# Projected query and key chunks by way of DRAM, a new layout of queries and keys, and another place for Wo in the last batch

## The chip, the cores and the metric

The kernel runs on one core of a Trainium2 chip. The metric is the device time of one execution, in microseconds (us), and the figure given is the median of the runs. A run of this kernel is timed to about 0.1%: its three runs lie between 1504.58 and 1505.42 us.

## The reference

One transformer layer, post-norm, on X of 4 batches x 1024 tokens x 512 channels, float32: causal attention with 16 query heads and 8 key/value heads of 64 (two query heads share one key/value head), rotary embedding on q and k, scores capped by a tanh, then an int8-quantised linear layer, each followed by a residual and a layer norm.

```python
q = q * cos + _rotate_half(q) * sin
k = k * cos + _rotate_half(k) * sin
att = jnp.einsum('bhqd,bhkd->bhqk', q, k) * 256.0 ** (-0.5)
att = SOFTCAP * jnp.tanh(att / SOFTCAP)
att = softmax(where(causal, att, -inf))
x = _layernorm(x + (att @ v).reshape(b, t, NH * HD) @ Wo)
q8, in_scale = per_token_quant_int8(x)
x = _layernorm(x + float16((q8 @ weight.T) * in_scale * w_scale + bias))
```

## The kernel before, in words

Precision: each large float32 operand is split in a high part, rounded to float32r, and a low part, the rest; a product is then two or three float32r matmuls.

The work goes by batch b (4) and, inside a batch, by unit u (4). A unit is two key/value heads with their four query heads; units are numbered m = 4b + u through the kernel (16). Three chunks of a unit are projected: x = 0 is k for all 1024 tokens, x = 1 and 2 are q for the first and the second 512. PE projects a chunk (`project`, L655), DVE applies the rotary embedding (`rope_read`, L1076 to L1091), ACT rounds the high part (`round_rope`, L901), DVE makes the low part (`rope_low`, L1097). The parts stand in `work_r`, two places that chunks use in turn. From there they must reach `qk` on other partitions: a score matmul contracts over 128 partitions that hold high and low parts of q below each other, against k copied twice. `put` (L400) does that with eight DMAs for one part of one chunk: L418 for k (32 partitions x 1024 elements, 128 KB each), L427 for q (32 x 512, 64 KB each). `qk` has two halves of 32 KB per partition, for even and odd units.

Attention of a unit takes 18 steps s, nine for each key/value head. At a step PE computes 2 banks of scores (`score`, L709), ACT does tanh and exp (L914, L919), POOL masks (L1317), DVE splits the probabilities (L1109, L1113), and PE weighs v with them three steps later (`weigh`, L735). Sums and outputs leave by ACT (L933), which has two buffers in turn, and by a store to `y_scratch` on SP's queue (`put_sums`, L507). The projections of the next unit lie between the steps. The orders of all engines are written out by hand; waits are on semaphores. `turns` and `chunk_at` say at which step which chunk is read, rounded and put; in the last unit of a batch they come one or two steps later.

At the end of a batch the divisors are read back (`load_div`, L456), inverted, stored (`store_inverse`, L462), read as rows (`load_rows`, L471), spread over partitions by PE (L755), and y, read back in tiles (`load_y`, L448), is scaled and multiplied with Wo (`project_out`, L777), followed by norms and the linear layer. Wo, high and low part of 2 MB each, is read from `wo_scratch`: the high part at step 11 of the last unit (L589), since it lies on the place of the first head of odd units in `qk`, the low part after the last score (L603). At the same time v of the next batch is projected (`project_v`, L677), whose weights `load_wv` (L495) brings, and x of the next batch is loaded and split in unit 2 (`load_x_turned`, L436; `split_x`, L864 and L1051).

SP issues nearly all DMAs, one after the other, and its waits stand in the same row. At the end of batches 0 to 2 ACT issues one put of eight. In the first batch `wo` is first made in `qk`'s odd half and stored (L554, L558), so puts of unit 1 wait for that (L406).

## Time and profile before

| what | value |
|---|---|
| median of 3 runs | 1504.92 us |
| the profiled execution's own time | 1501.25 us |
| its span, first to last instruction | 1499.3 us |
| PE busy (matmul) | 1322.7 us, 88% |
| DVE, ACT, POOL busy | 1096.8, 849.1, 380.8 us |
| granted TensorE clock, mean | 0.936 of full speed |
| DMA | 196.22 MB, mean 131 GB/s |
| longest DMA waits of PE | 28.4 us for qk, 31.4 us for rows |

The span is one execution, and the profiled one was shorter than the median of the runs by 3.67 us. Busy time says how much an engine did, not whether it set the time: for this the profile has the waits (who waited for whom), the timeline, and the chain of work that ended last, followed back from the last instruction. SPq and ACTq are the two queues on which DMAs are issued; an issue there occupies the queue, and the landing comes later.

### The profile page before, as it was taken

To read this page: it belongs to the slowest core of one execution; us is meant where nothing else is said; L and a number is where in the kernel's file an instruction comes from. 1 tells how busy PE (TensorE), PEld (TensorE's weight loads), DVE (VectorE), ACT (ScalarE), POOL (GpSimd) and SP (SyncE) were. 2 spreads that over 40 slices of the span, in tenths; PEclk is the share of its full clock that TensorE was granted. 3 is DMA by queue.
4 is the path that set the end of the run, shared out by engine and by line. 5 is a ranking of instruction groups with operands and counts; after the bars stand their busy time and mean duration, and the time that the engine had idled before them with its cause. 6 is when DMAs were issued, how large, how long until landed. Compare 5 with 4: busy or idle time off the path is not lost.

```text
span 1499.3 us, 17504 instructions
## 1 busy us (share of the span) xinstructions
PE 1322.7 (88%) x5824; PEld 963.7 (64%) x5840; DVE 1096.8 (73%) x1367; ACT 849.1 (57%) x952; POOL 380.8 (25%) x448
## 2 busy tenths in 40 slices
PE   6479999978988999897886999999599799999695
PEld 5357777656655777675664777767476477777463
DVE  4369888863677888885486888888258788888485
ACT  4167687752236777764223777687123577779232
POOL 2231111102552111110265112111036312111165
PEclk9789999989988999998998999999799899999896
DMA  7766445474513454547341454446642154343541
GB/s 280 261 205 160 103 129 144 113 211 123 156 50 87 115 139 109 155 96 244 95 133 47 98 137 117 103 144 186 181 123 78 56 137 103 102 110 103 149 109 42
DMA packets 120765, 196.22 MB, mean 131 GB/s; under 512 B 26466, under 2 KB 68964, under 8 KB 116836
## 3 DMA queue, kind: packets, MB, share of 16 engines
q1 hardware_dynamic: 114916, 185.14, 44.2%
q10 hardware_dynamic: 5760, 9.97, 2.0%
q8 instruction: 46, 0.75, 0.2%
q14 instruction: 43, 0.35, 0.1%
HBM read 89.39 MB, written 38.54 MB: 85 GB/s over the span
## 4 chain that ended last, share of the span: by engine, by line
PE 62%; DVE 10%; DMA 9%; SPq 7%; issue 5%; ACT 3%; POOL 3%; ACTq 1%; DVEq 0%; POOLq 0%
PE ps L735 21%; PE ps L655 15%; PE ps L709 14%; PE ps L777 6%; PE ps L677 4%; SPq L427 4%; DMA y_scratch<-sums 3%; DMA rows<-r_scratch 2%; DVE prob_hi L1109 1%; ACT probs L914 1%; DVE stats L1195 1%; DVE probs L1174 1%; DMA qk<-work_r 1%; DMA r_scratch<-inverse 1%; POOL rstd L1332 1%
## 5 line engine op out<-in xcount | busy, mean ns | idle before, releaser
L735 PE MATMUL ps<-prob_hi,v 128*65 128x512 f32 (+3 forms) x1280 | 415.1, 374 | 3.3 <-DVE prob_lo L1113 3.3
L914 ACT ACTIVATE probs<-ps 128x1024 f32<-128x1024 f32 x288 | 293.6, 1020 | 161.9 <-PE ps L709 159.2
L709 PE MATMUL ps<-qk 128*128 128x512 f32 (+1 forms) x1280 | 322.9, 379 | 54.2 <-DMA qk<-work_r 28.4
L1113 DVE TENSOR_TENSOR prob_lo<-probs,prob_hi 128x1024 fp32r<-128x1024 f32 x288 | 360.1, 1250 | 9.9
L1317 POOL TENSOR_SCALAR_AFFINE_SELECT probs<-probs 128x256 f32<-128x256 f32 (+1 forms) x192 | 145.3, 765 | 808.0 <-ACT probs L919 808.0
L919 ACT ACTIVATE probs<-probs 128x1024 f32<-128x1024 f32 x288 | 305.6, 1061 | 8.8
L709 PEld LDWEIGHTS ps<-qk 128*128 128x128 f32 x1280 | 230.1, 193 | 116.9 <-ACT probs L914 27.9
L655 PE MATMUL ps<-xT,w_ring 128*128 128x512 f32 x1152 | 293.5, 399 | 10.0 <-DVE xT L1051 8.0
L1109 DVE CAST prob_hi<-probs 128x1024 fp32r<-128x1024 f32 x288 | 206.3, 716 | 118.5 <-POOL probs L1317 69.6
L655 PEld LDWEIGHTS ps<-xT,w_ring 128*128 128x128 f32 x1152 | 219.6, 193 | 58.3 <-DVE xT L1051 9.3
L735 PE MATMUL ps<-prob_lo,v 128*65 128x512 f32 (+1 forms) x640 | 239.2, 374 | 0.0
L735 PEld LDWEIGHTS ps<-prob_hi,v 128*65 128x65 f32 (+1 forms) x1280 | 173.0, 136 | 92.5 <-DVE prob_lo L1113 5.7
L777 PE MATMUL ps<-wo,y_hi 128*128 128x512 f32 x512 | 184.9, 434 | 11.4 <-POOL y_lo L1323 11.4
L933 ACT ACTIVATE sums<-ps 65x512 f32<-65x512 f32 x128 | 74.7, 584 | 104.9 <-PE ps L735 87.7
L777 PEld LDWEIGHTS ps<-wo,y_hi 128*128 128x128 f32 x512 | 102.7, 205 | 48.0 <-POOL y_lo L1323 17.5
L677 PE MATMUL ps<-w_v,xT 128*128 128x512 f32 x384 | 97.9, 413 | 39.7 <-issue 27.9
L735 PEld LDWEIGHTS ps<-prob_lo,v 128*65 128x65 f32 x640 | 87.6, 137 | 51.6 <-issue 2.0
L1323 POOL TENSOR_TENSOR y_lo<-y_raw,y_hi 128x1024 fp32r<-128x1024 f32 x32 | 76.2, 2381 | 155.0 <-ACT y_hi L941 155.0
L677 PEld LDWEIGHTS ps<-w_v,xT 128*128 128x128 f32 x384 | 76.7, 202 | 58.7 <-issue 42.1
L777 PE MATMUL ps<-wo,y_lo 128*128 128x512 f32 x256 | 112.5, 439 | 0.0
L961 ACT ACTIVATE q16T<-ps 128x512 bf16<-128x512 bf16 x32 | 19.1, 597 | 112.2 <-PE ps L787 112.2
L941 ACT ACTIVATE y_hi<-y_raw 128x1024 fp32r<-128x1024 f32 x32 | 33.8, 1057 | 74.8 <-DVE y_raw L1137 74.8
(77 smaller groups left out, 1042.9 us busy)
## 6 DMA issues: line engine op xcount, KB each, us to landing
qk<-work_r SPq DMA_DIRECT2D x256, 128.0 KB, 2.3
qk<-work_r SPq DMA_DIRECT2D x488, 64.0 KB, 2.0
y_scratch<-sums SPq DMA_DIRECT2D x128, 130.0 KB
wo<-wo_scratch SPq DMA_DIRECT2D x8, 2048.0 KB, 7.8
y_raw<-y_scratch SPq DMA_DIRECT2D x64, 256.0 KB, 4.1
w_ring<-w_scratch SPq DMA_DIRECT2D x15, 1024.0 KB, 5.8
x_raw<-X_T SPq DMA_DIRECT2D x16, 512.0 KB, 5.1
x_in<-X SPq DMA_DIRECT2D x32, 256.0 KB, 2.9
```

Of the source, the lines that this page charges most:

```text
L655: mm = nc.tensor.matmul(ps[:, bank + n, :], w_ring[:, slot, w, k, :], xT[:, a, k, half * HT:(half + 1) * HT], start=(k == w == a == 0), st ...
L677: mm = nc.tensor.matmul(ps[:, v_bank(t), :], xT[:, a, k, t * P:(t + 1) * P], weights[:, w, k, :], start=(k == a == w == 0), stop=(k == KC ...
L709: mm = nc.tensor.matmul(scores[:, g % 2, col:col + REP * w].rearrange("p (h q) -> p h q", h=REP), qk[:, n % 2, i, 2 + part, keys], qk[:, n ...
L735: mm = nc.tensor.matmul(sums_ps[:, :, GQ - w:GQ], v[:, kt, v0:v0 + width], p[:, at, col:col + REP * w].rearrange("p (h q) -> p h q", h=REP ...
L777: mm = nc.tensor.matmul(bank, (y_lo[:, y_place(t), k, :] if a else y_hi[t % 2][:, k, :]), wo[:, w, k, :], start=(n == 0), stop=(n == 3 * K ...
L914: nc.scalar.activation(probs[:, prob_place(g), :], scores[:, g % 2, :], ACT.Tanh, scale=SCORE_SCALE / SOFTCAP).then_inc(capped, 1)
L919: nc.scalar.activation(probs[:, prob_place(g), :], probs[:, prob_place(g), :], ACT.Exp, scale=SOFTCAP).then_inc(exped, 1)
L933: nc.scalar.activation(sums[0:VJ, slot, :], ps[0:VJ, PV_BANK + c % 2, :], ACT.Copy).then_inc(sums_kept, 1)
L1109: nc.vector.tensor_copy(prob_hi[:, hi_place(g), :], probs[:, prob_place(g), :]).then_inc(rounded, 1)
L1113: nc.vector.tensor_tensor(prob_lo[:, prob_place(g), :], probs[:, prob_place(g), :], prob_hi[:, hi_place(g), :].bitcast(F32), ALU.subtract) ...
L1317: nc.gpsimd.affine_select(out=diag, in_=diag, compare_op=ALU.is_ge, fill=0.0, base=0, pattern=[[0, n], [1, P]], channel_multiplier=-1).the ...
L1323: nc.gpsimd.tensor_tensor(y_lo[:, y_place(t), :, :], y_raw[:, y_place(t), :, :], y_hi[t % 2][:, :, :].bitcast(F32), ALU.subtract).then_inc ...
```

## The change

`put` is gone. A part of a chunk now goes out with one DMA, `send`, from `work_r` to `chunk_scratch` in DRAM (512 KB), and comes back with `take`: four DMAs for k, two for q, 256 KB each, into 32 partitions. Takes wait for the landing of their send; DVE's reuse of `work_r` waits only for the send (`wait_sent`). All are on SP; ACT issues none. Takes of unit 1 are all issued in steps 15 to 17 of unit 0. In `qk` the four query heads of a unit now lie together, then k high for both heads, then k low, so that Wo's place there is free only after a batch's last score. For batches 0 to 2 both parts of Wo are loaded then, one before the sums of the last but one group and one after the rows of tile 1; in the last batch both go into the place of `xT` at steps 1 and 2 of the last unit. All four `load_wv` of the next batch are issued before the last chunk's send.

```diff
-        qk = sb("qk", [P, 2, 2, 4, T], F32R)
-        wo = over("wo", "qk", [P, 2, KO, C], F32R, skip=32 * KB)
+        qk = sb("qk", [P, 2, 2 * REP + 4, T], F32R)
+        wo_first = over("wo", "qk", [P, 2, KO, C], F32R, skip=32 * KB)
+        wo_last = over("wo_last", "xT", [P, 2, KO, C], F32R)
...
+            def load_wo(b, part):
+                if b == B - 1:
+                    sp.wait_ge(projected, chunks_upto(U - 1, 2))
+                sp.dma_start(wo_of(b)[:, part, :, :].rearrange("p k n -> p (k n)").bitcast(F32),
+                             wo_scratch[:, part * KO * C:(part + 1) * KO * C]
+                             ).then_inc((wo_hi_loaded, wo_lo_loaded)[part], 16)
...
+            def send(m, x, low):
+                sp.wait_ge(rope_lo if low else rope_hi, chunks_upto(m, x))
...
+                sp.dma_start(chunk_scratch[m % 2, x, low], work_r[:, place_of(m, x), 1 - low, :].bitcast(F32)
+                             ).then_inc(chunk_sent[place_of(m, x)][low], 16)
+
+            def take(m, x, low):
+                sp.wait_ge(chunk_sent[place_of(m, x)][low], 16 * ((3 * m + x) // 2 + 1))
...
+                if m == 1:
+                    sp.wait_ge(wo_stored, 32)
+                if m >= 2:
+                    sp.wait_ge(scored, unit_scored(m - 2))
...
+                for half in range(2):
+                    if x == 0:
+                        src = chunk_scratch[m % 2, 0, low, 64 * half:64 * (half + 1), :].rearrange("(i d) n -> d i n", i=2)
+                        for copy in range(2):
+                            r0 = 64 * copy + 32 * half
+                            sp.dma_start(qk[r0:r0 + 32, m % 2, 2 * REP + 2 * low:2 * REP + 2 * low + 2, :].bitcast(F32), src
+                                         ).then_inc(k_put[m % 2], 16)
+                    else:
+                        src = chunk_scratch[m % 2, x, low, :, half * HT:(half + 1) * HT].rearrange("(h d) n -> d h n", d=32)
+                        r0 = 64 * low + 32 * half
+                        sp.dma_start(qk[r0:r0 + 32, m % 2, 0:2 * REP, (x - 1) * HT:x * HT].bitcast(F32), src
+                                     ).then_inc(q_put[m % 2][x - 1], 16)
...
                         if u == UB - 1 and s == 14:
                             load_div(b, 0)
+                            if b + 1 < B:
+                                load_wv(b + 1, 2)
+                                load_wv(b + 1, 3)
                         if at := chunk_at(b, u, s, turns(u, 5, 10, 14)):
-                            put(sp, *at, 0)
-                        if (at := chunk_at(b, u, s, turns(u, 6, 11, 15))) and at != (UB * b + UB, 2):
-                            put(sp, *at, 1)
+                            send(*at, 0)
+                        if at := chunk_at(b, u, s, turns(u, 6, 11, 15)):
+                            send(*at, 1)
+                            if m > 1:
+                                take(*at, 0)
+                        if (at := chunk_at(b, u, s, turns(u, 7, 12, 16))) and m > 1:
+                            take(*at, 1)
+                        if m == 1 and s >= 15:
+                            take(1, s - 15, 0)
+                            take(1, s - 15, 1)
...
-                        if u == UB - 1 and s == 11:
-                            sp.wait_ge(scored, scores_upto(b, u * 2 * NS + NS - 1))
-                            sp.dma_start(wo[:, 0, :, :].rearrange("p k n -> p (k n)").bitcast(F32),
-                                         wo_scratch[:, 0:KO * C]).then_inc(wo_hi_loaded, 16)
+                        if b == B - 1 and u == UB - 1 and s in (1, 2):
+                            load_wo(b, s - 1)
...
-                for x in range(3):
-                    wait_put(sp, last, x)
+                wait_sent(sp, last, 2)
                 load_rows(b, 0)
-                sp.wait_ge(scored, scores_upto(b, NB - 1))
-                sp.dma_start(wo[:, 1, :, :].rearrange("p k n -> p (k n)").bitcast(F32),
-                             wo_scratch[:, KO * C:2 * KO * C]).then_inc(wo_lo_loaded, 16)
+                if b + 1 < B:
+                    sp.wait_ge(scored, scores_upto(b, NB - 1))
+                    load_wo(b, 0)
                 put_sums(b, NKV - 1, G - 2)
...
                 load_rows(b, 1)
+                if b + 1 < B:
+                    load_wo(b, 1)
...
-                if more:
-                    put(act, UB * b + UB, 2, 1)
```

How the change moves instructions is shown at three places, all on SP. A row is a line of the kernel, what is issued, the shape of one DMA and how often it comes in a row.

The start, from the load of Wo on; before:

```order
L534 DMA wo_raw<-L_attn_Wo 128x8x512
L418 DMA qk<-work_r 32x1024 x8
L481 DMA w_ring<-w_scratch 128x1024
L418 DMA qk<-work_r 32x1024 x8
L427 DMA qk<-work_r 32x512 x32
L486 DMA w_ring<-w_scratch 128x2048
```

The same place in the changed kernel (L491 is a send, L510 a take of k, L515 a take of q):

```order
L491 DMA chunk_scratch<-work_r 128x1024
L460 DMA w_ring<-w_scratch 128x1024
L491 DMA chunk_scratch<-work_r 128x1024
L510 DMA qk<-chunk_scratch 32x2x1024 x8
L491 DMA chunk_scratch<-work_r 128x1024 x2
L515 DMA qk<-chunk_scratch 32x4x512 x4
L491 DMA chunk_scratch<-work_r 128x1024 x2
L515 DMA qk<-chunk_scratch 32x4x512 x4
L465 DMA w_ring<-w_scratch 128x2048
```

48 issues in a row became 22, the weights of unit 1 in the same places between them.

The last steps of unit 0, batch 0, up to the loads for unit 2, in the changed kernel; before, these puts were spread over steps 5 to 15, eight at a time:

```order
L491 DMA chunk_scratch<-work_r 128x1024
L527 DMA y_scratch<-sums 65x512
L491 DMA chunk_scratch<-work_r 128x1024
L510 DMA qk<-chunk_scratch 32x2x1024 x8
L515 DMA qk<-chunk_scratch 32x4x512 x8
L527 DMA y_scratch<-sums 65x512 x2
L460 DMA w_ring<-w_scratch 128x1024
```

All sixteen takes of unit 1 stand behind the last of its six sends.

The end of batch 0, from the v weights on; before:

```order
L495 DMA w_v<-wv_scratch 128x1024 x2
L456 DMA div<-y_scratch 128x32
L495 DMA w_v<-wv_scratch 128x1024
L507 DMA y_scratch<-sums 65x512
L427 DMA qk<-work_r 32x512 x8
L495 DMA w_v<-wv_scratch 128x1024
L448 DMA y_raw<-y_scratch 64x8x128 x4
L456 DMA div<-y_scratch 128x32
L462 DMA r_scratch<-inverse 128x32 x2
L471 DMA rows<-r_scratch 2x8x128 x2
L603 DMA wo<-wo_scratch 128x4096
L507 DMA y_scratch<-sums 65x512
```

And in the changed kernel:

```order
L481 DMA w_v<-wv_scratch 128x1024 x2
L435 DMA div<-y_scratch 128x32
L481 DMA w_v<-wv_scratch 128x1024 x2
L527 DMA y_scratch<-sums 65x512
L491 DMA chunk_scratch<-work_r 128x1024 x2
L515 DMA qk<-chunk_scratch 32x4x512 x4
L427 DMA y_raw<-y_scratch 64x8x128 x4
L435 DMA div<-y_scratch 128x32
L441 DMA r_scratch<-inverse 128x32 x2
L450 DMA rows<-r_scratch 2x8x128 x2
L471 DMA wo<-wo_scratch 128x4096
L527 DMA y_scratch<-sums 65x512
```

The v weights stand before the last chunk, ACT's eight issues of its low part (not in SP's rows before) are now among SP's, and the load of Wo at that place is the high part; the low part follows after the rows of tile 1.

## Rows read from the trace of the kernel before

**Rows 1.** Page, part 4: the chain that ended last, shares by engine.

```profile
PE 62%; DVE 10%; DMA 9%; SPq 7%; issue 5%; ACT 3%; POOL 3%; ACTq 1%; DVEq 0%; POOLq 0%
```

**Rows 2.** Windows: start:end, length, busy us of each engine, PEclk, DMA share, GB/s.

```profile
65.00:70.00 5.00, 0.00 (x0) 0.00 (x0) 0.00 (x0) 0.00 (x0) 0.00 (x0) 0.50 0.97 234
251.00:258.00 7.00, 7.00 (x35) 5.00 (x34) 5.94 (x7) 6.97 (x9) 0.91 (x2) 1.00 0.80 236
341.00:346.00 5.00, 5.00 (x22) 3.25 (x21) 1.23 (x1) 1.72 (x3) 0.00 (x0) 1.00 0.99 368
175.00:233.00 58.00, 58.00 (x275) 43.13 (x274) 49.43 (x52) 43.61 (x48) 9.78 (x12) 1.00 0.46 119
```

**Rows 3.** DMA issues, whole run: count, KB each, median us from issue to landing.

```profile
qk<-work_r SPq DMA_DIRECT2D x256, 128.0 KB, 2.3
...
x_in<-X SPq DMA_DIRECT2D x32, 256.0 KB, 2.9
...
w_ring<-w_scratch SPq DMA_DIRECT2D x15, 512.0 KB, 3.9
```

**Rows 4.** Timeline of SP at the start: start us, us, operation, count.

```profile
59.68 5.03 SPq L418 DMA_DIRECT2D qk<-work_r  x8
...
70.50 21.60 SPq L427 DMA_DIRECT2D qk<-work_r  x32
```

**Rows 5.** Timeline of PE at the start; in brackets idle time before.

```profile
79.52 2.05 PE L709 MATMUL ps<-qk 128*128 128x512 f32 x6 [24.47 <-DMA qk<-work_r]
...
84.84 1.98 PE L655 MATMUL ps<-xT,w_ring 128*128 128x512 f32 x8
...
90.74 2.08 PE L709 MATMUL ps<-qk 128*128 128x512 f32 x4 [3.92 <-DMA qk<-work_r]
...
92.61 3.62 PE L655 MATMUL ps<-xT,w_ring 128*128 128x512 f32 x8
```

**Rows 6.** Timelines of DVE and of PE where unit 1 begins.

```profile
139.87 1.22 DVE L1097 TENSOR_TENSOR work_r<-work,work_r 128x1024 fp32r<-128x1024 f32 x1
...
142.33 1.10 PE L709 MATMUL ps<-qk 128*128 128x512 f32 x6
```

**Rows 7.** SP's timeline in unit 2 of batch 0, and the waits of the whole run.

```profile
257.85 4.95 SPq L427 DMA_DIRECT2D qk<-work_r  x8
262.84 0.59 SPq L436 DMA_DIRECT2D x_raw<-X_T  x1
...
PE ps L655 <- DVE xT L1051: 8.0, 3, 3.2
```

**Rows 8.** First batch's end: timelines of DVE, ACT, SP; the chain; landing of Wo.

```profile
322.02 1.22 DVE L1097 TENSOR_TENSOR work_r<-work,work_r 128x1024 fp32r<-128x1024 f32 x1
...
316.57 0.59 ACT L933 ACTIVATE sums<-ps 65x512 f32<-65x512 f32 x1 [1.24 <-DMA y_scratch<-sums]
...
331.94 2.62 SPq L448 DMA_DIRECT2D y_raw<-y_scratch  x4
...
339.61 0.57 SPq L471 DMA_DIRECT2D rows<-r_scratch  x2
...
340.62 7.34 DMA y_scratch<-sums
...
350.57 2.82 DMA rows<-r_scratch
...
354.71 7.88 PE ps L777 x24
...
DMA to landing us min/median/max: 7.3/8.4/9.6
```

**Rows 9.** Last batch's end: timeline of ACT, and the chain.

```profile
1353.00 0.57 ACT L933 ACTIVATE sums<-ps 65x512 f32<-65x512 f32 x1
...
1366.59 0.57 ACT L933 ACTIVATE sums<-ps 65x512 f32<-65x512 f32 x1
...
1397.18 7.52 DMA y_scratch<-sums
```

More of the change, by code:

```diff
@@ L325, in place_of, with wait_sent @@
             return (3 * m + x) % 2
[L327 to L329 removed]
+        def wait_sent(eng, m, x):
+            for low in range(2):
+                eng.wait_ge(chunk_sent[place_of(m, x)][low], 16 * ((3 * m + x) // 2 + 1))
         def prob_place(g):
@@ L535, in _ @@
             for x in range(3):
-                put(sp, 0, x, 0)
+                send(0, x, 0)
                 if x == 0:
@@ L539, in _ @@
                     load_wk(1)
-                put(sp, 0, x, 1)
+                send(0, x, 1)
+                take(0, x, 0)
+                take(0, x, 1)
             sp.wait_ge(projected, chunks_upto(0, 2))
```

79 lines of the change are left out of this document (30 added, 49 removed).

## The prediction, made blind

> **What bounds the kernel now.** I read the page first, its chain of work that ended last: PE makes 62% of it, DMA 9%, SP's queue 7% [rows 1]. A window over one steady head unit, 58 us, shows PE busy for all of it, DMA at 0.46 (last row of [rows 2]). So inside the 15 steady units a cheaper queue buys nothing: SP's 48 issues per unit lie under PE. What can move are places where PE stands. I looked for these in the waits and then in SP's and PE's timelines: the start (PE idle until 79.52), the begin of unit 1, the projection that waits for xT, the three batch ends, and the last batch's end.
>
> Two prices first. A put of eight DMAs occupies SP 5.03 us for 1 MB [rows 4], 0.63 us per issue, with 2.3 us from issue to landing [rows 3]. While k puts ran back to back, the DMA engines were 0.97 busy at 234 GB/s; a stretch of q puts and x loads gives 236/0.80 = 295, a pure 128-partition load 368 at 0.99 [rows 2]. So issue and bytes lie close together: here SP's issuing sets the pace. A rule speaks against the change: the Trainium skill (DMA: Bandwidth & Descriptors, Issuing engines are not separate DMA queues) says that issue time is usually small relative to the DMA. By it, removing issues would gain nothing at the start, and the sum would be 4.5 us worse.
>
> New operations: a send (512 KB, 128 partitions) and a take (256 KB into 32 partitions). Neither is in the trace. For a send I take 3.9 us to landing, the 512 KB w_ring load; for a take 2.9 us, the 256 KB x_in load [rows 3]; ends 2 and 5 us. Each costs one issue of 0.63 us. Per unit 48 issues become 22 (6 sends, 8 takes of k, 8 of q), bytes rise from 4 to 7 MB, which in a steady unit makes DMA 0.46 into some 0.8 at worst, still under PE: nothing. The new q and k layout feeds the same matmuls: nothing.
>
> **Start, -4.5 us.** Before, the first k put is issued at 59.68, q's second half ends its issuing at 92.1; PE gets its first score at 79.52, then waits 3.92 us for the second q half until 90.74 [rows 4, 5]. Now: k high sent 59.7; k low sent 63.3, when DVE has it; takes of k high 63.9 to 66.4, k low waits for its send and goes 67 to 69.5; q first half sent 69.5 to 70.7, landed 75 and 77, taken to 78.3, there at about 80.7 (1.2 us later than before). q second half sent 78.3, taken by 84.3, landed 87. PE needs it 7.3 us after its first score, at 88.0, against 90.74: 2.7 saved. Without the wait the clock stays up: the next 8 projections took 3.62 us after the wait and 1.98 before it [rows 5], the scores 2.08 against some 1.1, so up to 5.3 in all; DVE's next work covers part. Ends: -7 and 0.
>
> **Unit 1, +15 us.** This is the largest term and a loss. Before, unit 1's k and q were put while they became ready. Now the takes of unit 1 all stand behind the last send, in steps 15 to 17. That send waits for DVE's low part, which starts at 139.87 and ends at 141.1; PE was ready for unit 1's first score at 142.33 [rows 6]. SP then issues the send (141.8), 8 takes of k and 4 of q, 12 x 0.63 = 7.6 us, to 149.4, plus 2.3 landing: 151.7, a wait of 9.4. By bytes (3.67 MB with the send): at 234 GB/s 15.7 us, to 157.5, a wait of 15.2; at 368 issue decides. I take 155, a wait of 12.8, as the takes alternate between upper and lower partitions and read DRAM, and add 2.2 for the cold clock (as in rows 5: 2.6 for eight projections and four scores). Everything is queued behind that score on PE, so all of it is paid. Ends: +9.4 and +17.4. The second q half comes 2 steps later and is covered.
>
> **xT, -3.5 us.** In unit 2 of batches 0 to 2 the last x part is issued at 262.84 behind a put of eight at 257.85; PE waits 8.0 us in three times for xT [rows 7]. Now it stands behind one send and two takes, 3 x 0.63 instead of 8: 3.2 us earlier, minus 1 MB that lies ahead in the queue, and ACT's and DVE's own splits are late next. 1.2 each: 3.5. Ends: -7 and 0.
>
> **Three batch ends, -10 us.** The chain runs: DVE's low part (322.02 to 323.2), ACT's eight issues, landing, y loads, 1/sum stored, rows loaded at 339.61: 16.4 us after DVE [rows 8]. Now: the send, its landing 3.9 to 4.7 after its issue (the two takes of the high part go out meanwhile), two takes 1.3, and then the same stretch as from the first y load at 331.94 to the rows at 339.61, 7.7: 12.9 to 13.8. That is 2.6 to 3.5 us less, and I take 3.0. Further, Wo's high half no longer goes out at step 11 just ahead of a store of sums; that store held ACT for 1.24 us [rows 8]; I count it in two of three batches. Together 9.0 + 2.4 = 11.4; since 12 MB more are moved in each batch I take 10. The last w_v load is no longer behind a put, but PE then waits for the rows chain instead, so it brings nothing more. Behind the rows the 2 MB Wo half still slows a store of sums to 7.34 us [rows 8], as before. Both Wo halves now load after the last score. The low half is issued right behind the rows of tile 1, whose landing begins at 350.57; PE begins its 24 products at 354.71 and needs the low half after 16 of them, two thirds of 7.88, at 360.0: some 9.2 us after the issue. Wo lands in 7.3 to 9.6 [rows 8]: covered, barely. Ends: -16 and -4.
>
> **Last batch, -2.7 us.** Both halves are loaded early, into xT's place. The store of sums that took 7.52 us behind Wo's low half now takes the 2.9 us of a small load [rows 3, 9]: -4.6, of which I count 4.5. But 4 MB are issued behind the sums that ACT kept at 1353.00, from about 1354 on. At 7.5 us for 2 MB with sums behind them, and some 6 for the other 2 MB at 368 GB/s [rows 2, 9], they hold the queue, and with it the next sums, until 1368; ACT wants that sums buffer back at 1366.59: +1.8 with the store's own landing. Ends: -5 and +1.
>
> **Sum.** -4.5 + 15 - 3.5 - 10 - 2.7 = -5.7. The profiled execution took 1501.25 us (span 1499.3, so 1.95 around it), 3.67 under the median 1504.92; the sum against it is 1495.5, and against the median **1499.2**.
>
> **Rivals.** *A, only issues count (1490 us).* The takes' bytes hide under their issues. Unit 1 costs 9.4 + 2.2 = 11.6, the others reach further: -5.5 - 4 - 12.5 - 4.6; sum -15. For it: 368 GB/s in the Wo window, and that SP alone paced the puts. Against: k puts at 0.97 busy.
>
> *B, bytes count (1509 us, slower).* Takes that write 32 partitions run at the 234 GB/s of the puts. Unit 1 costs 15.2, 1 for the last landing and 2.2 for the clock = 18.4; at the start each MB of k takes 4.5 us, gain 1.5; xT 2.5; a batch end 2.7, so 8; last 2. Sum 18.4 - 1.5 - 2.5 - 8 - 2 = +4.4. It decides from about 240 GB/s down: there the gains no longer carry unit 1. For it: the busy share 0.97 in rows 2. Against: those puts also read 32 partitions, takes don't. The Trainium skill (SBUF — State Buffer, Door 1: The DMA port swizzle) has DMA bandwidth depend on how many of 16 ports the partitions reach, and 32 partitions reach 8 of them; by it takes run at half of its 436 GB/s, 218, and the time would be this rival's or 1 us more.
>
> *C, Wo comes too late (1509 us, slower).* Wo's low half lands 12.5 us after its issue instead of in time, since x rows, a sum load and the 1/sum store share the engines: 3.3 us at each of three ends, +10 on the sum, +4.2 in all. It decides from a landing of about 12 us (9.2, and 5.7 + 3 spread over three ends). For it: one landing of 9.6 is already seen; against: rows and y are ahead of it, x behind.
>
> *D, no change (1503 to 1506).* Unit 1's loss and the batch ends' gain cancel: the sum's terms need only err by 4 us.
>
> **Chances.** Forecast 0.42, A 0.20, B 0.20, C 0.08, D 0.10. A measurement of this kernel tells about 0.2% (3 us) from no change. Faster by over 3 us: 0.36 of the forecast's 0.42, plus A: 0.56. Within: 0.06 and D: 0.16. Slower: B and C: 0.28. Range: 1488 to 1512, from a little past A to past B.
>
> **What would show it.** On SP, 22 issues per unit. PE: first score near 80.7, no wait before the third; at the start of unit 1 a PE wait of about 13 us on the takes of k and q (9.4 for A, over 16 for B); xT waits under 5 us in total; at the batch ends rows of tile 0 issued 13 to 14 us after DVE's low part; Wo's low half not named among PE's waits (else C); the store of sums at the last end near 3 us. A steady unit should still last 58 us; if it is longer by more than 0.3 us, the whole account is wrong, as also if unit 1 starts without a wait.

## The result: 28 us slower, and the profile after

The changed kernel takes 1533.34 us (median of 4 runs, 1531.99 to 1535.42), against 1505.17 for the kernel before on the same chip (4 runs, 1504.58 to 1507.07). The ratio is 1.0186, 95% interval 1.0169 to 1.0204. I had predicted 1499.2 and a range of 1488 to 1512: outside, and on the wrong side. The profiled execution of after took 1535.42 us, its span 1533.3; the span of before was 1499.3, so the two traces differ by 34.0. Of these some 6 are the two executions: before's was 3.9 under its median here, after's 2.1 over.

The page of after, its busy times, the chain that ended last [rows 1] and the DMA issues [rows 3]:

```profile
PE 1330.5 (87%) x5824; PEld 969.2 (63%) x5840; DVE 1097.5 (72%) x1367; ACT 848.6 (55%) x952; POOL 379.0 (25%) x448
...
PE 59%; DMA 14%; DVE 10%; issue 6%; ACT 4%; POOL 3%; SPq 3%; ACTq 0%; DVEq 0%; POOLq 0%
...
qk<-chunk_scratch SPq DMA_DIRECT2D x256, 256.0 KB, 5.4
...
chunk_scratch<-work_r SPq DMA_DIRECT2D x96, 512.0 KB, 3.0
```

No engine has more instructions; PE's busy time is 7.8 us longer for the same 5824 matmuls, at a mean granted clock of 0.932 instead of 0.936. In the chain SP's queue falls from 7% to 3%, as meant, and DMA rises from 9% to 14%; 246.50 MB are moved instead of 196.22. A take lands in 5.4 us (median); the prediction had 2.9. The waits of PE say on what:

```profile
PE ps L737 <- DMA qk<-chunk_scratch: 54.8, 6, 29.4
PE ps L784 <- DMA rows<-r_scratch: 39.2, 11, 7.3
...
PE ps L737 <- issue: 16.1, 1, 16.1
```

L737 is the score matmul. Apart from the start's 29.4 there are 25.4 us in five waits for takes, and 16.1 more at the start of unit 1, which the profile puts down to "issue". The waits for xT (8.0 in [rows 7]) are gone.

**Where the 34 us come from.** ACT's tanh (L914 before, L943 after) comes 72 times per batch, 18 per unit; number g in one timeline less number g in the other tells how far after is behind at that point, and the increase between two points is what lies between them:

| stretch | g | lag at its ends, us | change | predicted |
|---|---|---|---|---|
| start and unit 0 | up to 17 | to 1.95 | +2.0 | -4.5 |
| start of unit 1 | 17 to 20 | 1.95, 22.14 | +20.2 | +15 |
| end of unit 2, first steps of unit 3, batch 0 | 53 to 57 | 22.19, 27.33 | +5.1 | -1.2 |
| the same, batch 1 | 125 to 129 | 25.92, 29.76 | +3.8 | -1.2 |
| the same, batch 2 | 197 to 201 | 28.99, 36.09 | +7.1 | -1.2 |
| rest of these units (sums held) | 57 to 71 and so on | | -2.7 | -2.4 |
| ends of batches 0 to 2, up to the next unit 2 | 71 to 125 and so on | | -2.1 | -7.6 |
| last unit | 269 to 287 | 33.46, 40.13 | +6.7 | +1.8 |
| last end | 287 to the end | 40.13, 34.0 | -6.1 | -4.5 |

They add up to 34.0 (with 0.05 between g 20 and 53). Of the start's 2.0, 1.2 is there before the first send: DVE begins to rotate unit 0's k at 59.69 instead of 58.48 (L1114 and L1087). Each row compares one execution with one. How far rows scatter is seen in experiments 2, 4, 6 and 9, wherever a stretch is untouched by their edits: the start of unit 1 costs 19.0 to 19.9 there, the three stretches with unit 3's first steps 4.6 to 6.0, 3.3 to 4.8 and 4.2 to 7.4, the batch ends together -2.7 to +2.8, the last unit 4.9 to 6.7. So 1 to 2 us in a row mean little, and the sign of the batch ends' -2.1 is not shown.

**The start.** SP's timeline [rows 4], with start, duration, operation and count:

```profile
64.53 0.32 SPq L491 DMA_DIRECT2D chunk_scratch<-work_r  x1
64.96 4.33 SPq L510 DMA_DIRECT2D qk<-chunk_scratch  x8
69.33 0.90 SPq L491 DMA_DIRECT2D chunk_scratch<-work_r  x2
78.17 1.99 SPq L515 DMA_DIRECT2D qk<-chunk_scratch  x4
80.20 0.90 SPq L491 DMA_DIRECT2D chunk_scratch<-work_r  x2
86.79 2.01 SPq L515 DMA_DIRECT2D qk<-chunk_scratch  x4
```

and the chain of the same stretch:

```profile
64.53 3.02 DMA chunk_scratch<-work_r
...
69.80 9.57 DMA chunk_scratch<-work_r
```

The issues are even cheaper than thought: eight takes in 4.33 us, 0.54 each, a send 0.32 to 0.45. But a send that lands in 3.02 us when the queue is empty needs 9.57 behind the takes of k: over 2 MB, seven takes and another send, are still ahead of it. SP waits for that landing before it can take the low part of q. PE's first score comes at 85.71 (PE's timeline, idle time in brackets), where I had 80.7 and before had 79.52 [rows 5]:

```profile
85.71 2.04 PE L737 MATMUL ps<-qk 128*128 128x512 f32 x6 [29.45 <-DMA qk<-chunk_scratch]
...
94.77 1.22 PE L737 MATMUL ps<-qk 128*128 128x512 f32 x4 [1.80 <-DMA qk<-chunk_scratch]
```

**Unit 1** [rows 6], SP's timeline and then PE's:

```profile
144.27 0.33 SPq L491 DMA_DIRECT2D chunk_scratch<-work_r  x1
144.69 4.31 SPq L510 DMA_DIRECT2D qk<-chunk_scratch  x8
149.11 3.70 SPq L515 DMA_DIRECT2D qk<-chunk_scratch  x8
```

```profile
161.73 2.05 PE L737 MATMUL ps<-qk 128*128 128x512 f32 x6 [16.09 <-issue]
```

From the send at 144.27 to the score at 161.73 are 17.5 us, in which the 3.67 MB that I had counted land: 210 GB/s. SP had issued the last take that this score needs (the twelfth) by 151.0 or so; 10 us later its data was there. That is no matter of issues, whatever name the wait bears. The windows (columns as in [rows 2]):

```profile
66.00:77.00 11.00, 0.00 (x0) 0.00 (x0) 4.88 (x5) 1.06 (x1) 0.00 (x0) 0.50 1.03 254
150.00:158.00 8.00, 0.00 (x0) 0.00 (x0) 0.22 (x1) 0.00 (x0) 0.00 (x0) 0.53 1.04 228
158.00:164.00 6.00, 2.27 (x7) 2.01 (x8) 0.00 (x0) 0.18 (x1) 0.00 (x0) 0.50 1.07 222
209.00:267.00 58.00, 58.00 (x273) 43.11 (x272) 49.41 (x52) 43.61 (x48) 9.75 (x12) 1.00 0.61 173
```

While takes run, the DMA engines are busy all the time (share 1.0) at 222 to 254 GB/s. The landings say the same: of unit 1's eight takes of k the first lands 4.0 us after its issue and the last 8.3, of its takes of q the last 13.7; the eight puts of k high before had all landed 2.3 to 2.4 us after theirs. The last row is a steady unit: still 58 us with PE full; DMA rose from 0.46 to 0.61.

**The last unit of batches 0 to 2.** The prediction had nothing there. SP's timeline in unit 2 of batch 0:

```profile
279.20 0.33 SPq L491 DMA_DIRECT2D chunk_scratch<-work_r  x1
281.41 0.80 SPq L515 DMA_DIRECT2D qk<-chunk_scratch  x2
282.26 0.43 SPq L415 DMA_DIRECT2D x_raw<-X_T  x1
282.73 0.51 SPq L465 DMA_DIRECT2D w_ring<-w_scratch  x1
284.35 1.00 SPq L515 DMA_DIRECT2D qk<-chunk_scratch  x2
```

The last two takes, the low part of q's second half, are issued behind a piece of x and 1 MB of weights for q. PE needs them at the third step of the next unit and waits 6.7, 6.1 and 7.1 us for them in batches 0 to 2. In the last unit of the last batch the weights aren't loaded any more, but with no projections between its steps the third step comes some 3.6 us earlier; PE waits 3.7.

**End of batch 0** [rows 8], SP's timeline, then the chain:

```profile
355.28 2.01 SPq L515 DMA_DIRECT2D qk<-chunk_scratch  x4
...
367.42 0.55 SPq L450 DMA_DIRECT2D rows<-r_scratch  x2
```

```profile
349.36 7.14 DMA chunk_scratch<-work_r
...
368.40 7.64 DMA y_scratch<-sums
...
379.01 9.06 DMA wo<-wo_scratch
```

DVE's low part ends at 349.33; its send needs 7.14 us to land, for two loads of v weights (1 MB) and the other send stand before it. Rows go out at 367.42, 18.1 us after DVE, against 16.4 before and 12.9 to 13.8 in the prediction. And then comes the landing of Wo's low half, 9.06 us from its issue. This is no wait of 9 us: PE works on the sixteen products that need only the high half until 388.04, and starts the other eight at 388.11, some 0.2 us later than they would have followed. At this end the v weights did come sooner for PE: over the three ends its waits before them (`project_v`, put down to "issue") fell from 27.9 to 9.7 us, while those for the rows rose from 31.4 to 39.2.

### The profile page after: what moved, and what is told of

Its sections match the earlier page's. It is cut to its first block, busy times and chain, and to the rows that moved or that the text cites. A ratio compares the mean times of both kernels' runs of the same rounds, so it can differ in the third digit from the quotient of the medians.

```text
span 1533.3 us, 17160 instructions
## 1 busy us (share of the span) xinstructions
PE 1330.5 (87%) x5824; PEld 969.2 (63%) x5840; DVE 1097.5 (72%) x1367; ACT 848.6 (55%) x952; POOL 379.0 (25%) x448
## 2 busy tenths in 40 slices
DMA packets 126394, 246.50 MB, mean 161 GB/s; under 512 B 19810, under 2 KB 62308, under 8 KB 122468
## 4 chain that ended last, share of the span: by engine, by line
PE 59%; DMA 14%; DVE 10%; issue 6%; ACT 4%; POOL 3%; SPq 3%; ACTq 0%; DVEq 0%; POOLq 0%
PE ps L764 20%; PE ps L683 15%; PE ps L737 14%; PE ps L806 5%; DMA chunk_scratch<-work_r 4%; PE ps L705 4%; DMA qk<-chunk_scratch 3%; DMA rows<-r_scratch 2%; DMA y_scratch<-sums 2%; ACT probs L943 1%; DVE prob_hi L1136 1%; DMA wo<-wo_scratch 1%; DMA r_scratch<-inverse 1%; ACT probs L948 1%; DVE probs L1201 1%
## 5 line engine op out<-in xcount | busy, mean ns | idle before, releaser
L737 PE MATMUL ps<-qk 128*128 128x512 f32 (+1 forms) x1280 | 327.6, 384 | 96.9 <-DMA qk<-chunk_scratch 54.8
L943 ACT ACTIVATE probs<-ps 128x1024 f32<-128x1024 f32 x288 | 293.7, 1020 | 205.3 <-PE ps L737 202.5
L737 PEld LDWEIGHTS ps<-qk 128*128 128x128 f32 x1280 | 233.0, 196 | 160.8 <-issue 47.2
L806 PE MATMUL ps<-wo,y_hi 128*128 128x512 f32 x384 | 137.0, 430 | 9.0 <-POOL y_lo L1350 8.5
L705 PE MATMUL ps<-w_v,xT 128*128 128x512 f32 x384 | 103.5, 431 | 21.4 <-DVE w_v L1235 11.7
L705 PEld LDWEIGHTS ps<-w_v,xT 128*128 128x128 f32 x384 | 80.5, 212 | 42.8 <-issue 24.7
L806 PEld LDWEIGHTS ps<-wo,y_hi 128*128 128x128 f32 x384 | 75.4, 201 | 36.3 <-POOL y_lo L1350 12.4
L806 PE MATMUL ps<-wo,y_lo 128*128 128x512 f32 x192 | 82.3, 429 | 0.0
```

The lines of the kernel that those rows point to most:

```text
L705: mm = nc.tensor.matmul(ps[:, v_bank(t), :], xT[:, a, k, t * P:(t + 1) * P], weights[:, w, k, :], start=(k == a == w == 0), stop=(k == KC ...
L737: mm = nc.tensor.matmul(scores[:, g % 2, col:col + REP * w].rearrange("p (h q) -> p h q", h=REP), qk[:, n % 2, 2 * REP + 2 * part + i, key ...
L806: mm = nc.tensor.matmul(bank, (y_lo[:, y_place(t), k, :] if a else y_hi[t % 2][:, k, :]), wo_of(b)[:, w, k, :], start=(n == 0), stop=(n == ...
L943: nc.scalar.activation(probs[:, prob_place(g), :], scores[:, g % 2, :], ACT.Tanh, scale=SCORE_SCALE / SOFTCAP).then_inc(capped, 1)
```

## The experiments

Experiments 8 and 12 are edits of the kernel before, all others of the changed one. "Lag at g" is the table's measure, against the trace of before. The kernels ran in several sessions; each ratio is to the kernel before in the same session (medians 1502.8 to 1506.4), and where two kernels are compared in us, it is by their ratios, 0.0010 being 1.5 us. In these sessions single runs of the kernel before spread from 1497.9 to 1511.6, so the 95% intervals given are 0.1 to 0.4% to either side.

**1. The same takes into 128 partitions.**

```diff
-                            r0 = 64 * copy + 32 * half
-                            sp.dma_start(qk[r0:r0 + 32, m % 2, 2 * REP + 2 * low:2 * REP + 2 * low + 2, :].bitcast(F32), src
+                            cols = slice(copy * HT, (copy + 1) * HT)
+                            src = chunk_scratch[m % 2, 0, low, :, cols]
+                            sp.dma_start(qk[:, m % 2, 2 * REP + 2 * low + half, cols].bitcast(F32), src
...
-                        r0 = 64 * low + 32 * half
-                        sp.dma_start(qk[r0:r0 + 32, m % 2, 0:2 * REP, (x - 1) * HT:x * HT].bitcast(F32), src
...
+                        src = chunk_scratch[m % 2, x, low, :, half * HT:(half + 1) * HT]
+                        sp.dma_start(qk[:, m % 2, 2 * low + half, (x - 1) * HT:x * HT].bitcast(F32), src
...
```

> Takes write 128 partitions instead of 32: same count, same bytes, same waits, but the parts land in another arrangement, so the scores are computed from q and k in the wrong places. Theory P (a take is slow because it writes only 32 partitions, some 215 to 250 GB/s): the 3.67 MB before unit 1 go at 340 to 370 GB/s, PE's wait there falls from 16.1 us to 9 to 11 (then the issues decide), the waits at the third step of the last units (6.7, 7.1 us) fall under 3, and the whole is 15 to 25 us under the changed kernel's 1533: 1508 to 1518. Theory D (reading DRAM, or the extra bytes of the sends, is slow, whatever is written): nothing moves by more than 3 us, 1530 to 1536.

The kernel leaves out the arrangement that the scores need, so its values are not the layer's; instructions, bytes and waits are the same.

Measured: 1507.63 us, ratio to before 1.0024 [0.9999, 1.005]; 24 of the 28 us are gone. Its windows, at the start and in unit 1; the wait at unit 1; and the takes' row of the DMA issues:

```profile
65.00:75.00 10.00, 0.00 (x0) 0.00 (x0) 5.23 (x6) 1.06 (x1) 0.00 (x0) 0.50 0.99 342
144.00:152.00 8.00, 0.06 (x1) 0.10 (x1) 0.47 (x1) 0.00 (x0) 0.00 (x0) 0.50 1.00 363
```

```profile
PE ps L736 <- issue: 12.0, 1, 12.0
```

```profile
qk<-chunk_scratch SPq DMA_DIRECT2D x256, 256.0 KB, 4.2
```

342 and 363 GB/s instead of 254 and 228, at a DMA share of 1 in both kernels. The edit also changes what a take of k reads (64 rows of 4 KB, now 128 of 2 KB), but not what a take of q reads: 128 rows of 2 KB in both. While only takes of q run, the rate is 398 GB/s (149 to 153 us in this trace) against 222 (158 to 164 in the changed kernel's). So the takes' rate hangs on the partitions written. The Trainium skill (SBUF — State Buffer, Door 1: The DMA port swizzle) has 32 partitions reach 8 of 16 ports, and half of its 436 GB/s is 218. The trace agrees: 228 and 222 where takes run alone, 2 to 5% over it; 254 holds sends as well, and they read 128 partitions. But 12.0 us remain of the wait at unit 1, more than the 9 to 11 expected: there even fast takes come too late, as they are all issued at once. At the third step of units 3 PE still waits 3.2, 4.1 and 3.9 us, not under 3.

**2. Takes of unit 1 spread over the steps, as in the later units.**

```diff
-                            if m > 1:
-                                take(*at, 0)
-                        if (at := chunk_at(b, u, s, turns(u, 7, 12, 16))) and m > 1:
+                            take(*at, 0)
+                        if at := chunk_at(b, u, s, turns(u, 7, 12, 16)):
...
-                        if m == 1 and s >= 15:
-                            take(1, s - 15, 0)
-                            take(1, s - 15, 1)
```

> The takes of unit 1 stand at the steps where those of all later units stand. Theory (their place behind the last send is the loss at unit 1, tanh of its first step comes 16.6 us late and that of its second 3.6 more): both waits go, 1533 falls by 18 to 20, to 1513 to 1515. Rival (DRAM path too slow for one unit's time anyway, or Wo's store holds them): falls by less than 8, 1525 or more.

Measured: 1513.84 us, 1.0056 [1.0034, 1.0079], 20 us under the changed kernel. The lag at g 20 is 2.80 instead of 22.14. The moment at which these takes are issued is the largest single place of the loss, and it can be had back without a faster take.

**3. The weights of q behind the last takes of unit 2.**

```diff
-                            if s == 15:
-                                load_wq(m + 1)
+                        if u == 2 and b + 1 < B and s == 17:
+                            load_wq(m + 1)
```

> In unit 2 of batches 0 to 2 the 1 MB load of the next q weights goes out after the last take instead of before it. Theory (the last q part is late in units 3 because 0.5 MB of x and 1 MB of weights lie ahead of its take in the same queue): the waits of 6.7 to 7.1 us there shrink by 1 MB at 350 GB/s = 3 us each, together 8 to 10: 1523 to 1525. Rival (the take waits for its send's landing, not for bytes ahead of it): 1531 to 1535.

Measured: 1524.03 us, 1.0126 [1.0095, 1.0157], 9 less than the changed kernel. PE's wait in the last unit of batch 0:

```profile
PE ps L737 <- DMA qk<-chunk_scratch: 4.6, 1, 4.6
```

and 4.1 and 5.5 in batches 1 and 2: 4.6, 4.1 and 5.5 instead of 6.7, 6.1 and 7.1. The steps from g 53 to 57, 125 to 129 and 197 to 201 cost 3.8, 2.1 and 6.2 instead of 5.1, 3.8 and 7.1. That is 3.9 of the 10.0 by which the two traces differ. Of the rest 1.1 is there by g 17, before the edit acts, 3.0 lie between g 143 and 197 and 1.8 in the last unit, where nothing was edited, and that much is scatter (above). Of the three stretches the first two lie below the scatter of the unedited ones, the third inside it. So the 1 MB of weights ahead makes about 2 us of the first two waits, not the 3 expected, and the third doesn't show it; the larger part stays. The time falls in the expected range, but the account reaches only 4 of the 9 us.

**4. Wo of the last batch at steps 3 and 8 instead of 1 and 2.**

```diff
-                        if b == B - 1 and u == UB - 1 and s in (1, 2):
-                            load_wo(b, s - 1)
+                        if b == B - 1 and u == UB - 1 and s in (3, 8):
+                            load_wo(b, s // 8)
```

> In the last batch the two 2 MB loads of Wo go out at steps 3 and 8 of the last unit instead of 1 and 2. Theory (these 4 MB share the engines with the last q takes, so that PE waits 3.7 us for them, and hold back a store of sums; tanh loses 6.6 us between steps 1 and 7): 4 to 7 us less, 1526 to 1529. Rival (the takes were late by themselves, the loads cost nothing): 1531 to 1535.

Measured: 1532.05 us, 1.0177 [1.0136, 1.0218]: not to be told from the changed kernel. PE still waits 2.8 us there (3.7 in the changed kernel, 3.5, 3.5 and 3.2 in experiments 2, 6 and 9, which leave Wo alone), though the first load of Wo is now issued behind this score. My account fell, its rival held: the take comes too late for this step by itself, and the two loads of Wo have little to do with it.

**5. No way by DRAM: eight direct DMAs per part on SP, when the part is ready; layout, Wo and v weights as in the change.**

```diff
-                sp.dma_start(chunk_scratch[m % 2, x, low], work_r[:, place_of(m, x), 1 - low, :].bitcast(F32)
-                             ).then_inc(chunk_sent[place_of(m, x)][low], 16)
...
+                for i in range(2):
+                    for half in range(2):
+                        if x == 0:
+                            src = work_r[64 * half + 32 * i:64 * half + 32 * (i + 1), place_of(m, x), 1 - low, :].bitcast(F32)
+                            for copy in range(2):
+                                r0 = 64 * copy + 32 * half
+                                sp.dma_start(qk[r0:r0 + 32, m % 2, 2 * REP + 2 * low + i, :].bitcast(F32), src
+                                             ).then_inc(k_put[m % 2], 16)
...
```

> The way by DRAM is undone: each part goes straight to the new places of qk by eight DMAs, as before, when it is ready; the new layout, Wo's late load in batches 0 to 2 and its early load in the last, and the early load of the v weights stay. Theory (the loss is all in send and take: one queue, bytes into 32 partitions, and the late takes of unit 1): the start, unit 1 and units 3 are as in the kernel before, the end of the last batch keeps its gain of 6, so 1496 to 1503 where the kernel before takes 1504. Rival (Wo's late load at three batch ends costs its share): 1507 or more, with PE waiting on wo.

Measured: 1493.33 us (5 runs, 1491.78 to 1500.29), 0.9934 [0.9912, 0.9955]. That is under the 1496 to 1503 expected. So the way by DRAM costs 38 us, and what else the change does is worth 10. Its profiled execution was one of two long ones (1499.73), so that its lags (2.15 at g 17, 5.99 at g 57, 3.71 at g 287) lie above what its median would give. At the end of batch 0 the landing of Wo's low half lies on the chain here as well, and PE waits 0.26 us for it:

```profile
354.50 10.29 DMA wo<-wo_scratch
```

**6. At the start, four sends before any take.**

```diff
-                take(0, x, 0)
-                take(0, x, 1)
+                if x == 1:
+                    for y in range(2):
+                        take(0, y, 0)
+                        take(0, y, 1)
+            take(0, 2, 0)
+            take(0, 2, 1)
```

> At the start the first four sends go out before any take; all else as in the changed kernel. Theory (q's sends land 8.8 us after their issue because 2 MB of k takes lie ahead in the queue): the first tanh, 6.2 us late in the changed kernel, comes 3 to 4 us earlier, the third step comes no earlier than 2 us: 1529 to 1532. Rival (k's takes alone set the first score): nothing moves, 1531 to 1535.

Measured: 1534.79 us, 1.0201 [1.0181, 1.0221]. The first score comes at 84.20 instead of 85.71, so the first tanh is 1.5 us earlier and not 3 to 4; the lag at g 4 fell from 2.97 to 0.44. The total doesn't show it: this stands against a ratio that is 0.0015 higher, within the intervals. Inconclusive for the kernel. For the start it says that the sends' place behind the takes of k makes 1.5 of the 5 us by which the first score was late against the prediction; the rest stays with the sends ahead.

**7. Experiments 2, 3, 4 and 6 together.**

> Unit 1's takes at their steps, q weights after the takes, Wo of the last batch at steps 3 and 8, the four sends first: the four edits together. If they add up, 20 + 9 + 1 + 2 = 32 come off 1533: 1500 to 1504, the same as the kernel before within 0.3%. If the edits trade places (the queue only holds the bytes somewhere else), 1508 or more.

Measured: 1506.45 us (12 runs), 1.0018 [1.0004, 1.0032], between the two ranges expected. Order alone takes back 25 of the 28 us, and yet the way by DRAM stays no better than the kernel before, 13 above experiment 5. The lag is 1.87 at g 53 and 10.13 at g 287: it still grows in the last unit of batches 0 (4.7) and 2 (5.8).

**8. Kernel before, with the two parts of the change that stand apart:** the last v weights ahead of the last put, and both halves of Wo in `xT`'s place in the last batch (steps 3 and 8).

```diff
+        wo_last = over("wo_last", "xT", [P, 2, KO, C], F32R)
...
                         if u == UB - 1 and s == 14:
                             load_div(b, 0)
+                            if b + 1 < B:
+                                load_wv(b + 1, 2)
+                                load_wv(b + 1, 3)
...
-                        if u == UB - 1 and m < U and s in (14, 15):
-                            load_wv(b + 1, s - 12)
-                        if u == UB - 1 and s == 11:
+                        if b == B - 1 and u == UB - 1 and s in (3, 8):
+                            part = s // 8
...
+                        if b < B - 1 and u == UB - 1 and s == 11:
...
```

> The kernel before with direct puts and the old layout, and only two parts of the change: the v weights' last loads ahead of the last put, and both Wo halves of the last batch read early, into xT's place (at steps 3 and 8). Theory: the last batch's end gives 5 to 6 us, the three batch ends 0 to 3 together, as PE there waits for the rows chain: 1495 to 1499 against 1504. Rival (the gain at the end in the changed kernel came from the chain by way of DRAM): 1502 to 1505.

Measured: 1496.18 us, 0.9944 [0.9927, 0.996]. From g 287 to the end it gains 6.4, as the changed kernel does (6.1): this is Wo's new place.

**9. The k takes of the start on two queues:** ACT issues those into partitions 64 to 127, SP the others.

```diff
-                        for copy in range(2):
+                        for copy in range(1 if m == 0 else 2):
...
+            for low in range(2):
+                act.wait_ge(chunk_sent[0][low], 16)
+                for half in range(2):
+                    src = chunk_scratch[0, 0, low, 64 * half:64 * (half + 1), :].rearrange("(i d) n -> d i n", i=2)
+                    act.dma_start(qk[64 + 32 * half:96 + 32 * half, 0, 2 * REP + 2 * low:2 * REP + 2 * low + 2, :].bitcast(F32), src
+                                  ).then_inc(k_put[0], 16)
```

> In the changed kernel the start's k takes into partitions 64 to 127 (four of eight) are issued by ACT, idle there, those into partitions 0 to 63 by SP. Theory P (32 partitions written at a time are the limit; two queues write to both sides at once): while both run the rate rises from some 240 GB/s to over 300, and the first tanh comes 2 to 4 us earlier than in the changed kernel (it is 6.2 late against before). Rival (the DMA engines share one rate whatever the queue): the rate stays under 260 and the first tanh within 1 us.

Measured: 1531.18 us (2 runs), 1.0186 [1.0143, 1.0229]. The windows, start of the takes and what follows:

```profile
66.00:71.00 5.00, 0.00 (x0) 0.00 (x0) 1.49 (x2) 0.00 (x0) 0.00 (x0) 0.50 0.98 314
71.00:77.00 6.00, 0.00 (x0) 0.00 (x0) 4.23 (x5) 1.06 (x1) 0.00 (x0) 0.50 0.95 231
```

314 GB/s for 5 us, then 231, a mean of 269 against 254 with one queue. In the 5 us a 512 KB send runs too, which reads 128 partitions (issued at 65.67, landed at 70.24). The first tanh comes 6.29 us after before's where the changed kernel has 6.19, and the lag at g 4 is 2.09 instead of 2.97. It speaks rather for the rival; two runs settle nothing.

**10. Experiments 1 and 2 together.**

> Takes into 128 partitions (q and k arrive in another arrangement, so the scores are computed from wrong places) and unit 1's takes at their steps: the two largest losses of the changed kernel at once. The wide takes left unit 1 a wait of 12 us, which now goes too: 1507 - 12 = 1494 to 1497, some 8 under the kernel before. Rival (the remaining loss is the DRAM way's latency): 1503 or more.

The scores are of wrong places here as in experiment 1.

Measured: 1494.38 us, 0.994 [0.9914, 0.9966], 37 under the changed kernel. The lag is -1.5 at g 18 and 4.33 at g 287. With 128 partitions written and unit 1's takes spread, the same number of DMAs and the same bytes come to where the direct way of experiment 5 is. So rate and moment of the takes together are the whole loss, though PE still waits 3.5 to 4.5 us for takes in each of the units 3 of batches 0 to 2.

**11. The last two v weight loads behind the last send and its first takes.**

```diff
-                            if b + 1 < B:
-                                load_wv(b + 1, 2)
-                                load_wv(b + 1, 3)
...
+                            if u == UB - 1 and s == 16:
+                                load_wv(b + 1, 2)
+                                load_wv(b + 1, 3)
```

> In the changed kernel the last two loads of v weights, 1 MB, go out after the last send and the takes of its high part instead of before them. Theory (at a batch end the last send lands 7.1 us after its issue because those loads lie ahead of it, so that the rows of tile 0 go out 18.1 us after DVE's low part): the landing falls to 4 us or less, the rows come 2 to 3 us earlier, and three ends give 3 to 8 us: ratio 1.013 to 1.017 instead of 1.0186. Rival (the bytes only change places, since the w_v loads then hold back the low takes and the y loads): the rows come within 1 us of where they were and the ratio stays at 1.017 to 1.020.

Measured: 1540.28 us, 1.0229 [1.0203, 1.0254], 6.5 us slower than the changed kernel. At the end of batch 0 the chain, SP's timeline and PE's:

```profile
346.58 5.89 DMA chunk_scratch<-work_r
```

```profile
369.33 0.55 SPq L450 DMA_DIRECT2D rows<-r_scratch  x2
```

```profile
362.57 4.54 PE L705 MATMUL ps<-w_v,xT 128*128 128x512 f32 x12 [13.05 <-issue]
```

The row of the chain is the send of the high part, 5.89 us where it took 8.1; that of the low part, issued at 350.05, lands in 3.6 instead of 7.14, as expected. But the bytes only change places: the loads of y and divisors now stand behind the v weights, rows go out 19.3 us after DVE (350.03) instead of 18.1, and PE waits 13.05 us for the v weights where it waited 4.83. The rival's mechanism held, but the ratio lies above its 1.017 to 1.020: PE's longer wait had no price in it. The place of the v weights in the change is right.

**12. Experiment 8, and at the start ACT issues 16 of the 48 direct puts** (k's second copy, and the low part of q's first half).

```diff
-                put(sp, 0, x, 0)
+                put(sp, 0, x, 0, (0,) if x == 0 else (0, 1))
...
-                put(sp, 0, x, 1)
+                if x != 1:
+                    put(sp, 0, x, 1, (0,) if x == 0 else (0, 1))
...
+            round_rope(0, 0)
+            put(act, 0, 0, 0, (1,))
+            round_rope(0, 1)
+            put(act, 0, 0, 1, (1,))
+            put(act, 0, 1, 1)
+            round_rope(0, 2)
...
```

> The two parts of e9 with direct puts, and at the start, where SP's 48 issues of 0.63 us set the first score, ACT issues the k puts of the second copy and the low part of the first q chunk, 16 of 48. Theory (issue bound there): the first score comes 4 us or more earlier, limited by 3 MB at 240 GB/s, and the whole is 3 to 5 under e9's ratio 0.9944: 0.991 to 0.993. Rival (bytes bound already): within 1 us of e9.

Measured: **1491.82 us** (6 runs, 1490.46 to 1495.25), 0.9927 [0.9905, 0.9948]: faster than before and after. Windows and PE's timeline at the start:

```profile
65.00:70.00 5.00, 0.00 (x0) 0.00 (x0) 0.82 (x1) 0.00 (x0) 0.00 (x0) 0.50 1.00 279
70.00:75.00 5.00, 0.31 (x1) 0.34 (x2) 1.82 (x2) 0.00 (x0) 0.00 (x0) 0.50 0.97 285
```

```profile
74.69 2.05 PE L720 MATMUL ps<-qk 128*128 128x512 f32 x6 [18.98 <-DMA qk<-work_r]
```

The first score comes at 74.69 against 79.52; the lag at g 4 is -4.44, where experiment 8 has +0.38. That issuing set the pace before shows in the landings: the puts issued from 70.5 to 82, 0.63 us apart, landed 1.9 to 2.5 us after their issue, so none waited for bytes. The rate rose from 234 GB/s [rows 2] to 279 and 285. But here each queue also writes a half of its own, SP partitions 0 to 63 and ACT 64 to 127, and in both kernels the window 65 to 70 holds the w_ring load into 128 partitions; what of the rate is due to the second queue's issuing and what to the halves isn't separated. By the medians alone the two versions are not told apart (their intervals overlap); the timelines tell them apart there.

## Why the prediction was wrong

**Which steps failed.** Two. The first is the price of a take: "for a take 2.9 us", and, in unit 1, 13.2 us for 3.67 MB, which is 278 GB/s. The 2.9 us came from a 256 KB load into 128 partitions; the takes write 32. Those 3.67 MB took 17.5 us, 210 GB/s. Takes ran at 222 to 254 GB/s with full DMA engines, and at 342 to 363 when 128 partitions were written (experiment 1); in unit 1 they landed 4.0 to 13.7 us after their issue. The window with 0.97 and 234 GB/s [rows 2] was not as pure as the prediction took it: besides k puts it holds the 512 KB w_ring load (issued at 64.82, landed 5.4 us later). Before that load the puts landed 2.3 us after each issue, so "SP's issuing sets the pace" was right for the puts. It was wrong to carry it to takes, which bring 256 KB per issue of 0.54 us, where a put of k brought 128 KB in 0.63.

The second is the term put at nothing: "still under PE: nothing", for the additional bytes in a steady unit. It is the larger error: the three places at xT and units 3 were to give 3.5 us and cost 16.1, half of the 39.7 us between the sum of -5.7 and the 34.0 measured. With bytes doubled by the way through DRAM and one queue in order, all that stands behind a group of takes is late: a send by 6.6 us at the start (9.57 against 3.02). Order alone takes back 25 of the 28 us (experiment 7), the takes' width alone 24 (experiment 1), width and unit 1's order together 37 (experiment 10).

**Start, predicted -4.5, measured +2.0.** By the first step, apart from the 1.2 us that were there before. The wait before the third group of scores fell (3.92 to 1.80), but did not go as predicted, and the first score came 5 us later than predicted: k's eight takes land 3.8 to 8.3 us after their issue, and q's sends behind them. With q's sends ahead of them (experiment 6) the first score is 1.5 us earlier.

**Unit 1, predicted +15, measured +20.2.** Mechanism right, with the wait on the send and twelve takes; a size was off. The wait is 16.1 instead of 12.8 (rival B had 15.2 + 1), PE came to it 1.4 later than before, and 2.7 remain for the clock (granted 0.50, the level of 1.2 GHz, in the idle time) where I had 2.2. Experiment 2 shows the place of the takes to be the cause.

**xT, predicted -3.5.** The three waits for xT are gone, and in their stead stand 16.1 us in the next unit. That is the term missing from the prediction, the second largest cost and the largest error: I said that in steady units the additional bytes cost nothing, because the DMA share stays under 1. The mean share is 0.61 and the unit's 58 us are right. But the part that is due first lies behind x and weights in the same queue, and has 3 steps until PE asks for it. I looked at the share of a stretch where I had to look at the last transfer in it. Experiment 3 takes back about 2 us of the first two waits; with 128 partitions written (experiment 1) the same stretches cost 1.5, 1.3 and 4.4 us (11.59 to 13.06 and so on) instead of 5.1, 3.8 and 7.1, so most of the rest is the rate.

**Batch ends, predicted -10 with the held sums, measured -4.8.** The sums held as computed, -2.7 against -2.4. The rows chain was to be 12.9 to 13.8 us and is 18.1: the send's landing was taken as 3.9 to 4.7 and is 7.14, and the stretch from the first load of y to the rows was taken as 7.7 and is 10.0 (357.38 to 367.42). That Wo's low half would be "covered, barely" held: it landed 9.06 us after its issue, and PE lost some 0.2 us by it at this end; over the three ends the profile has three waits for it, of PE and its weight loads together, 1.8 us in all. What the longer chain costs wasn't separated, and these stretches scatter by as much as their change (see the table). Experiment 11 shows that a later load of v weights brings the send's landing sooner (3.6 us), but not the rows.

**Last batch, predicted -2.7, measured +0.6.** The last end is right: the store of sums is out of the chain there, -6.1 against -4.5. The last unit costs 6.7 instead of 1.8 (4.9 to 6.7 in experiments 2, 6 and 9): the late take again (3.7 wait), which I had not seen, and not Wo's 4 MB (experiment 4).

**The rivals.** B named the right cause, with a price that was too low: it gave unit 1 18.4 (20.2 measured), and still counted gains at start, xT and batch ends that don't come when each send also lands late. The rule of the port swizzle that I cited beside B was the better guide; "those puts also read 32 partitions, takes don't" was the argument that I let outweigh it, and experiment 1 refutes it. A fell, C fell (9.06 us and not 12), D fell.

**What stays open.** Of experiment 5 three executions lie at 1492 to 1493 and two at 1500; why isn't known. Why the gain of 2.5 us at g 4 in experiment 6 doesn't arrive at the end isn't settled, nor whether takes on two queues would be faster for long (experiment 9), nor whether the higher rate of experiment 12 comes from the second queue or from writing to both halves at once.

## What to carry to other kernels

Price a transfer by its bytes and the number of partitions at its SBUF side, from a row with the same number of partitions, and then look at what is queued behind it. Whether issues or bytes set the pace is read from the landings: if each comes as long after its issue as the last (2.0 us for q's puts at the start before), it is the issues; if they grow along the row (3.8 to 8.3 us for k's takes), it is the bytes, and fewer issues gain nothing. A way through DRAM doubles the bytes and adds a landing that the queue waits for: each piece must be fetched when its send has landed, ahead of big loads that nobody waits for yet, never all at once when the consumer is already there. A mean DMA share below 1 excludes no wait; the transfer that is due first decides.

## What the runs showed of the hardware

- Takes from DRAM into 32 partitions, rows of 2 and 4 KB: 222 to 254 GB/s with the DMA engines full; the same bytes to 128 partitions: 342 to 363. For takes of q alone, which read the same rows in both: 222 and 398.
- The busy share does not tell whether bytes are moved fast: it was 1.07 at 222 and 1.00 at 363 GB/s.
- A 512 KB send lands in 3.0 us on an empty queue, in 7.1 to 9.6 behind some 1.5 to 2.4 MB.
- An issue is not of one price: 0.32 us for one alone, 0.46 to 0.54 in a row of takes, 0.63 in a row of direct puts.
- With a second queue that took 16 of 48 copies within SBUF, each queue writing its own half of the partitions, the rate at the start rose from 234 to 279 and 285 GB/s and the first score came 4.8 us earlier, although the busy share had been 0.97 before.
